# Linear attention with butterfly FFN on one core: second batch's keys taken by VectorE, down butterfly spread over slots 1 to 14, x in 2 KB pieces, first slots reordered

## What is computed

```python
q, k, v = split(x @ W_qkv)                      # per head: 64 wide
q = relu(q @ W_f + b_f);  k = relu(k @ W_f + b_f)
kv = sum_n k[n]^T v[n];  norm = q . sum_n k[n] + 1e-6
x1 = layernorm(x + concat(q @ kv / norm) @ W_out + b_out)
h  = gelu(butterfly(x1 @ W_exp + b_exp, up_weights) + up_bias)
y  = butterfly(h, down_weights) @ W_con + b_con + down_bias
out = layernorm(x1 + y)
```

## Time and profile before

| what | us |
|---|---|
| median of 3 runs (lowest, highest) | 335.33 (334.68, 337.5) |
| the profiled execution | 335.18 |
| its span in the profile | 333.3 |
| TensorE busy in the span | 312.0 (94%) |
| VectorE busy | 242.5 (73%) |
| ScalarE busy | 160.1 (48%) |
| GpSimd busy | 88.0 (26%) |

### The profile page before, as it was taken

One profiled execution on the slowest core, in us unless ns is written; L12 is line 12 of the kernel. 1 busy time (PEld: TensorE's weight loads), 2 busy tenths in 40 slices (PEclk: granted clock), 3 DMA queues, 4 the chain that ended last, 5 costly groups with the idle time before them and its releaser, 6 DMA issues.

```text
span 333.3 us, 5119 instructions
## 1 busy us (share of the span) xinstructions
PE 312.0 (94%) x1813; PEld 218.1 (65%) x1813; DVE 242.5 (73%) x480; ACT 160.1 (48%) x284; POOL 88.0 (26%) x100
## 2 busy tenths in 40 slices
PE   4999799999989999999999999999999898999882
PEld 4876467766757767676777776667777666454471
DVE  2659999868599999778872996397839626477645
ACT  2633245444544445454542656346848845341351
POOL 4059999970000002100200220023004103111222
PEclk9999999999999999999999999999999999999998
DMA  6993244566701900730092006600380390840102
GB/s 181 267 314 132 78 150 154 163 219 148 171 2 38 219 0 5 180 74 0 7 208 46 0 3 147 140 0 2 99 192 3 78 209 6 189 125 2 31 1 63
DMA packets 25616, 33.72 MB, mean 101 GB/s; under 512 B 4184, under 2 KB 14456, under 8 KB 25592
## 3 DMA queue, kind: packets, MB, share of 16 engines
q1 hardware_dynamic: 25432, 33.38, 38.5%
q10 hardware_dynamic: 160, 0.03, 0.0%
HBM read 31.04 MB, written 2.36 MB: 100 GB/s over the span
## 4 chain that ended last, share of the span: by engine, by line
PE 74%; DVE 12%; DMA 4%; issue 4%; ACT 2%; SPq 2%; POOL 1%; POOLq 0%; DVEq 0%; ACTq 0%
PE ring L605 26%; PE kx_ps L692 12%; PE attn_ps L605 8%; PE ring L790 6%; PE ring L712 4%; PE attn_ps L742 4%; PE desk L614 3%; DMA x<-_L_ffn_down_weights_dram 2%; PE desk L726 2%; PE desk L701 2%; DVE qn L1274 2%; PE ring L672 1%; SPq L479 1%; DVE late L1160 1%; DMA q<-in_L_attn_W_qkv_dram 1%
## 5 line engine op out<-in xcount | busy, mean ns | idle before, releaser
L957 ACT ACTIVATE q<-ring,bf_col 128x512 f32<-128x512 f32 x64 | 43.8, 685 | 44.5 <-PE ring L605 43.7
L557 POOL TENSOR_TENSOR var_eps<-mean_var,ln_eps 128x4 f32<-128x4 f32 x14 | 7.1, 505 | 210.8 <-DVE mean_var L1287 210.8
L692 PE MATMUL kx_ps<-k,xs 128*128 128x512 f32 x128 | 60.1, 592 | 0.0
L943 ACT ACTIVATE qn_h<-qn 128x512 fp32r<-128x512 f32 x48 | 29.5, 625 | 27.7 <-DVE qn L1274 27.7
L1274 DVE TENSOR_TENSOR qn<-q,recips 128x512 f32<-128x512 f32 x64 | 41.0, 680 | 1.6 <-DMA recips<-recip_rows 1.6
L549 POOL TENSOR_TENSOR y<-hid,y_up 128x512 f32<-128x512 f32 x18 | 33.7, 1891 | 16.4 <-DMA hid<-in_L_ffn_up_weights_dram 15.4
L605 PE MATMUL ring<-xT_h,wq_h 128*128 128x512 f32 x64 | 35.5, 555 | 0.0
L692 PEld LDWEIGHTS kx_ps<-k,xs 128*128 128x128 f32 x128 | 23.9, 189 | 17.7 <-issue 15.4
L1142 DVE TENSOR_TENSOR qn_l<-qn,qn_h 128x512 fp32r<-128x512 f32 x48 | 32.1, 678 | 4.5 <-ACT qn_h L943 4.3
L1240 DVE TENSOR_TENSOR k_total<-k_total,k 128x1024 f32<-128x1024 f32 x24 | 34.8, 1449 | 0.6 <-ACT k L950 0.4
L1214 DVE TENSOR_TENSOR k<-ring,bf_minus 128x512 f32<-128x512 f32 x32 | 21.9, 684 | 16.5 <-PE ring L605 16.5
(11 more groups left out here) (176 smaller groups left out, 576.8 us busy)
## 6 DMA issues: line engine op xcount, KB each, us to landing
recips<-recip_rows SPq DMA_DIRECT2D x64, 256.0 KB, 5.2
hid<-in_L_ffn_up_weights_dram SPq DMA_DIRECT2D x9, 512.0 KB, 4.2
x<-_L_ffn_down_weights_dram SPq DMA_DIRECT2D x9, 512.0 KB, 6.1
xs<-in_L_attn_x_dram SPq DMA_DIRECT2D x4, 512.0 KB, 6.3
out_dram<-y SPq DMA_DIRECT2D x7, 256.0 KB, 4.0
q<-in_L_attn_W_qkv_dram SPq DMA_DIRECT2D x2, 512.0 KB, 7.3
q<-in_L_attn_W_qkv_dram SPq DMA_DIRECT2D x2, 256.0 KB, 3.5
q<-in_L_attn_W_out_dram SPq DMA_DIRECT2D x2, 256.0 KB, 8.3
```

The source lines that it names most:

```text
L692: t_.matmul(kx_ps[half], xs[b % XBUF][:, t, :], k[kt % KRING][:, half * CH:(half + 1) * CH], start=t == 0, stop=t == TILES - 1).then_inc(s ...
L943: a_.activation(dst, src, ACT.Copy).then_inc(done, 1)
L957: a_.activation(q[:, i % QRING, :], bank(("q", i))[:, :], ACT.Relu, bias=bf_col[:, :])\
```

## The change

1. BARE goes from 16 to 8: batch 1's 16 key halves too have no bias matmul and are taken by k_max on VectorE, and batch 1's kx and key sum end as batch 2's do.
2. The nine down steps lie in slots 1, 2, 3, 5, 6, 8, 10, 12, 14 (before: 1, 2, 3, 5, 6, 7, 8, 9, 10). Steps from PS_LAST (7) on use GpSimd's term buffers `term_up`. The bias steps move from slots 10 to 13 to 13 to 15, their transpose from 14 to 16. By L191 x of (2, 1), transposed in slot 14, now goes to the desk.
3. The copies of V and of all four vo parts go to ScalarE.
4. x and out are seen with four tokens on a partition in a row, so pieces are 2 KB and not 512 B.
5. The start: half of x of batch 0 is loaded first and transposed first; b_f's row is loaded from ScalarE's queue; slot 0 takes over the second half of x and the transposes of the q weights, and project_k(1, 0) comes ahead of their folds.

```diff
-    DOWN_STEP_SLOT = {1: 0, 2: 1, 3: 2, 5: 3, 6: 4, 7: 5, 8: 6, 9: 7, 10: 8}
+    DOWN_STEP_SLOT = {1: 0, 2: 1, 3: 2, 5: 3, 6: 4, 8: 5, 10: 6, 12: 7, 14: 8}
-    BIAS_SLOT = {10: [0, 1], 11: [2, 3], 12: [4, 5], 13: [6]}
-    BIAS_T_SLOT = 14
+    BIAS_SLOT = {13: [0, 1], 14: [2, 3], 15: [4, 5, 6]}
+    BIAS_T_SLOT = 16
...
-    BARE = 2 * TILES
+    BARE = TILES
...
-    xs_view = x.rearrange("b (t p) c -> b p t c", p=128)
-    out_view = out.rearrange("b (h t p) c -> (b h) p t c", p=128, h=CHUNKS)
+    xs_view = x.rearrange("b (h p t) c -> b p h t c", p=128, h=CHUNKS)
+    out_view = out.rearrange("b (h p t) c -> (b h) p t c", p=128, h=CHUNKS)
...
+            load_x(0, slice(0, 1), s_xs0)
             for half in range(2):
                 cols = slice(HD + half * CH, HD + (half + 1) * CH)
                 sp.dma_start(wqkv_raw[:, cols], W_qkv[:, cols]).then_inc(s_wk[half], 16)
-            sp.dma_start(xs[0][:, :, :], xs_view[0, :, :, :]).then_inc(s_xs[0], 16)
-            sp.dma_start(bf_row[:, :], b_f.rearrange("(o n) -> o n", o=1).to_broadcast([128, D])).then_inc(s_bf, 16)
+            load_x(0, slice(1, 2), s_xs[0])
...
             pe.wait_ge(s_const, 2)
+            pe.wait_ge(s_xs0, 16)
+            transpose_tiles(kx_ps[0], lambda i: xs[0][:, i, :]).then_inc(s_xp, 1)
             transpose_weights(2, ring[0]).then_inc(s_wT, 1)
             transpose_weights(3, ring[1]).then_inc(s_wT, 1)
...
-            pe.wait_ge(s_xs[0], 16)
-            transpose_tiles(kx_ps[0], lambda i: xs[0][:, i, :]).then_inc(s_xp, 1)
-            transpose_tiles(kx_ps[1], lambda i: xs[0][:, QUADS + i, :]).then_inc(s_xp, 1)
-            transpose_weights(0, desk).then_inc(s_dmade, 1)
-            transpose_weights(1, ring[2]).then_inc(s_wT, 1)
-            pe.wait_ge(s_wh, 2)
-            pe.wait_ge(s_wl, 2)
+            pe.wait_ge(s_wh, 1)
+            pe.wait_ge(s_wl, 1)
...
+                if s == 0:
+                    pe.wait_ge(s_xs[0], 16)
+                    transpose_tiles(kx_ps[1], lambda i: xs[0][:, QUADS + i, :]).then_inc(s_xp, 1)
+                    pe.wait_ge(s_wh, 2)
+                    pe.wait_ge(s_wl, 2)
                 for kt in k_tiles(s)[:1]:
                     project_k(kt, 1)
                 if s == 0:
+                    transpose_weights(0, desk).then_inc(s_dmade, 1)
+                    transpose_weights(1, attn_ps).then_inc(s_wT, 1)
+                    project_k(1, 0)
...
+                if s in V_SLOT:
+                    act.wait_ge(s_dmade, desk_of["v", V_SLOT[s]] + 1)
+                    a_.activation(wT[:, (4 + V_SLOT[s]) * CH:(5 + V_SLOT[s]) * CH], desk[:, :],
+                                  ACT.Copy).then_inc(s_dtaken, 1)
...
                 if s == 3:
-                    act.wait_ge(s_fold, 5)
-                    a_.activation(vo[:, 0:4, :].rearrange("p a m -> p (a m)"), attn_ps[:, :], ACT.Copy).then_inc(s_voa, 1)
+                    for half, fold in enumerate([attn_ps, spare_ps]):
+                        act.wait_ge(s_fold, 5 + half)
+                        a_.activation(vo[:, 4 * half:4 * half + 4, :].rearrange("p a m -> p (a m)"), fold[:, :],
+                                      ACT.Copy).then_inc(s_voa, 1)
...
+                if n >= PS_LAST:
+
+                    dve.wait_ge(s_up, 3 * STAGES)
+                    terms = term_up
```

More of the change, by code:

```diff
@@ L421, in weights, with load_x @@
                 sp.dma_start(wqkv_raw[:, cols], W_qkv[:, cols]).then_inc(done, 16)
+            def load_x(b, chunks, done):
+                dst = xs[b][:, :, :].rearrange("p (h t) c -> p h t c", h=CHUNKS)
+                sp.dma_start(dst[:, chunks, :, :], xs_view[b, :, chunks, :, :]).then_inc(done, 16)
+            load_x(0, slice(0, 1), s_xs0)
             for half in range(2):
@@ L453, in _ @@
             load_down(0)
-            sp.dma_start(xs[1][:, :, :], xs_view[1, :, :, :]).then_inc(s_xs[1], 16)
+            load_x(1, slice(0, CHUNKS), s_xs[1])
+            for h in range(2):
+                sp.dma_start(bf_col[h * D:(h + 1) * D, :], b_f.rearrange("(p o) -> p o", o=1)).then_inc(s_bfc, 16)
             load_down(1)
@@ L954, in q_relu @@
                 act.wait_ge(s_made, ring_of["q", i] + 1)
+                if i == 0:
+                    act.wait_ge(s_bfc, 32)
                 if i >= QRING:
@@ L1027, in yT_copy @@
                 a_.activation(yT[:, :], bank(("down", n))[:, :], ACT.Identity, bias=bdn_col[:, :]).then_inc(s_taken, 1)
+            act.wait_ge(s_xp, 1)
+            hi(xT_h[:, 0, 0:CH], kx_ps[0], s_xTh)
             act.wait_ge(s_wT, 1)
             a_.activation(wT[:, 2 * CH:3 * CH], ring[0][:, :], ACT.Copy).then_inc(s_wTa, 1)
[L1031 to L1036, removed]
+            act.wait_ge(s_fold, 1)
+            hi(wk_h[:, 0:CH], attn_ps[:, :], s_wh)
+            act.wait_ge(s_bf, 16)
             act.wait_ge(s_bfz, 1)
@@ L1073, in _ @@
                 if s == 0:
-                    for half, fold in enumerate([attn_ps, spare_ps]):
+                    act.wait_ge(s_wT, 3)
+                    a_.activation(wT[:, CH:2 * CH], attn_ps[:, :], ACT.Copy).then_inc(s_wTa, 1)
+                    k_relu(1, 0)
+                    for half, fold in enumerate([spare_ps, attn_ps]):
                         act.wait_ge(s_fold, half + 3)
@@ L1325, in _ @@
             v.memset(wout_diag, 0.0).then_inc(s_zero, 1)
+            dve.wait_ge(s_xTh, 1)
+            lo(xT_l[:, 0, 0:CH], kx_ps[0], xT_h[:, 0, 0:CH], s_xTl)
             dve.wait_ge(s_wT, 2)
             v.tensor_copy(wT[:, 3 * CH:4 * CH], ring[1][:, :]).then_inc(s_wTd, 1)
-            for half, fold in enumerate([attn_ps, spare_ps]):
-                cols = slice(half * CH, (half + 1) * CH)
-                dve.wait_ge(s_wh, half + 1)
-                lo(wk_l[:, cols], fold[:, :], wk_h[:, cols], s_wl)
-            dve.wait_ge(s_xTh, 1)
-            lo(xT_l[:, 0, 0:CH], kx_ps[0], xT_h[:, 0, 0:CH], s_xTl)
+            dve.wait_ge(s_wh, 1)
+            lo(wk_l[:, 0:CH], attn_ps[:, :], wk_h[:, 0:CH], s_wl)
             dve.wait_ge(s_bfh, 2)
```

61 lines of the change are left out of this document (29 added, 32 removed).

## The result

The changed kernel takes 356.68 us (median of 4 runs, 355.97 to 357.84), the kernel before, on the same chip, 335.25. The ratio is 1.0613, 95% interval 1.0567 to 1.0658. The change costs 21.4 us; I had forecast 7.2 (342.5, range 336 to 346.5). The sign and the places were right, the size was a third of what came. Runs over 1.5% above the fastest of their own kernel are left out of the ratios, though not of the medians: 1119.53 us once in f1, 354.42 in f2, 340.08 in f4.

What follows compares the result with a forecast made beforehand. TensorE bounds the whole, but VectorE, nearly full too, sets the pace in slots 4 to 16. Slot 17 comes 7.6 us later (143.3, not 135.7), the last store gives back 0.3: 335.2 + 7.6 - 0.3 = 342.5 us, range 336 to 346.5.

Steps and rivals of the forecast that it cites:

- a sum that gave 142.6: Slot 17 of TensorE: VectorE's start 49.8, plus work 82.5, idle time 9.8 and 0.5 us.
- a walk that gave 144.0: Slots 4 to 16 followed slot by slot in code order, with waits of both engines; slot 17 at 144.0 us.
- Term (d), the start: Start of the kernel: transposing half of x before the weights wins 0.5 us, bounds -1.5 and +1.
- VectorE's work: Slots 4 to 16: 82.5 us, up from 71.7, with k_max at 0.60 us each, or 1.13 for eight beside GpSimd.
- The queue step: Slots 8 to 10, SyncE: spread(0) waits behind load_down(7), beginning near 77.5 us; normalise_q(0) starts at 85.5 to 86.5.
- the list of signs: What would show the forecast right or wrong, among them VectorE over 90% busy in slots 12 to 16.
- VectorE's idle time: Slots 4 to 16: waits for norm, recips and key products, 2.5 + 2.3 + 3.1 + 1.9 = 9.8 us.
- What TensorE saves: Bias matmuls 3.7, V wait 1.7, slot 11 wait 1.4, start 0.5, last store 0.3: 7.6 us if VectorE followed.
- Rival 1: Slots 4 to 16: VectorE packs, idle about 3 us or less, slot 17 near 135 or earlier; chance 0.10.
- rival 2: Slots 4 to 16: VectorE idle 3 to 6 us, slot 17 at 136 to 139, time 335 to 338; chance 0.16.
- Rival 3: Late throughout: k_max slowed beside GpSimd (+4.2), key weights late at the start (+2), 347 to 349 us; chance 0.06.
- Rival 4: The bias products stay, or VectorE's part is wholly hidden in idle time; no chance of its own given.

Runs made afterwards that it cites:

- f1: Changed kernel with the second batch's keys back on ScalarE (BARE 16) and down and bias steps in their old slots: 334.93 us, ratio 0.9955.
- f2: Changed kernel with load_down(7) moved behind spread(0) in SyncE's list, nothing else: 351.59 us, ratio 1.0388.
- f4: Kernel before, with only the V and vo copies on ScalarE and x and out in 2 KB pieces: 336.59 us, ratio 1.0004.
- e4: Changed kernel with the start of before (x of batch 0 whole, behind the key weights): 355.24 us, ratio 1.0557.
- e1: Changed kernel with 59 matmuls that nobody reads put into TensorE's stalls in slots 4, 11, 15 and 16: 350.56 us, ratio 1.0412.
- g3: Kernel before, with only the second batch's keys moved to VectorE (BARE 8, constants made in slot 3): 345.1 us, ratio 1.0273.
- e2: Changed kernel with the second batch's keys back on ScalarE with the bias matmul (BARE 16), thinned steps kept: 350.06 us, ratio 1.0415.
- g1: Changed kernel with BARE 16, thinned steps kept, load_down(7) behind spread(0) and down step 8 in slot 13: 341.07 us, ratio 1.0134.
- g2: Changed kernel with down steps 5 and 6 in slots 7 and 9 and step 8 in slot 13: 345.3 us, ratio 1.0265.
- g4: f1 with down step 8 in slot 11 instead of 10: 333.45 us, ratio 0.9918 against the kernel before.

## Why the prediction was right in kind and wrong in size

I had slot 17 of TensorE at 143.3, between a sum that gave 142.6 and a walk that gave 144.0; it began at 156.48. From there the delay was carried to the end as I had said: 20.8 us at slot 17, 21.9 in the profiled execution. Of the 13.9 us beyond the sum, 4.0 are in VectorE's start, 1.2 in its work and 8.5 in its idle time, together 13.7.

**Term (d), the start: wrong.** I took 0.5 us won (bounds -1.5 and +1). Slot 1 came 2.45 later. The 256 KB of x ahead of the key weights pushed the second half of these from 5.45 to 8.36, and TensorE, full before from there on, waited 2.76 us for it. That is 3 us off the term and outside its bounds. A part of it is chance: in the ten profiles with the new start slot 1 begins between 20.5 and 22.3 (half of them before 21.5), in the four with the old one between 19.4 and 20.5, so the usual loss is nearer 1.7. In the time e4 won back 1.4 us. That the 256 KB on the DMA engines are what holds the key weights up is argued, not shown.

**VectorE's start of slot 4: 53.77, not 49.8.** In e4, with the old start, the same k_max starts at 51.81, so 2.0 of the 4.0 come from the new start; the other 2.0 I haven't traced.

**VectorE's work: right.** 82.5 us forecast for slots 4 to 16, 83.67 measured. k_max takes 684 ns on average over all 48, and 0.68 and 0.69 at 53.77 and 60.69, where GpSimd is busy. So the price of 0.60 start to start, and not the bound of 1.13, holds. As in the prediction, this agrees with the rule of the Trainium skill, SBUF — State Buffer, section Who interferes with whom, by which a VectorE instruction with one SBUF input doesn't contend with GpSimd: k_max has one source in PSUM and one in SBUF.

**The stalls of TensorE: right, where they had a price.**

| where | forecast | measured |
|---|---|---|
| slot 4, k_max behind down step 2 | 3.6 | 4.17 |
| slot 11, step 6 ahead of add_attn(0) | 4 | 4.40 |
| slot 10, the desk behind m_lo(0,0) | named, no price | 1.97 |
| slot 15, x(2,1) at the desk | 4 | 4.47 |
| slot 16, the copy of wdn | 3 | 2.19 |
| wait of VectorE for recips | 2.6 to 3.6 | 3.10 |

The queue step was right in kind: spread(0) stood behind load_down(7) and started 5.0 us behind the reciprocal at 79.40 (SyncE's queue in the changed kernel, to set beside the earlier trace rows); the walk had 5 us between them (72.5 to 77.5), the list of signs 3 to 4:

```profile
84.40 1.82 SPq L478 DMA_DIRECT2D recip_rows<-recip  x4
```

One sign was missed narrowly: VectorE was busy 42.83 of 48.70 us from slot 12 to 16, 88% and not over 90%. The first up product came at 164.84, not at about 150.

**VectorE's idle time: the step that failed.** I wrote "Idle in all 2.5 + 2.3 + 3.1 + 1.9 = 9.8 us" and had only the latencies of norm, the recips and a key product in two places in it. Measured up to the copy of wdn it is 18.3 us (101.95 us from 53.80 to 155.75, less 83.67 of work). The forecast waits all came: 1.79 for norm (2.5 forecast), 2.42 ahead of slot 10 (2.3), 3.10 for the recips (3.1), 3.27 in slot 11 (1.9). What the sum lacks is first of all VectorE waiting for key products right behind the stall of slot 4 (timeline of VectorE in the changed kernel):

```profile
60.69 0.69 DVE L1245 TENSOR_TENSOR k<-ring,bf_minus 128x512 f32<-128x512 f32 x1 [4.03 <-PE ring L612]
```

I had let TensorE catch up at once after each stall, at 0.23 us a matmul. In truth it ran at 0.42 for some microseconds behind each long stall, and so VectorE, which had just been what TensorE waited for, now waited for TensorE. The product for the 4.03 us wait began its last matmul 5.7 us behind the end of the stall (54.50 to 60.22); in e1, where the stall was filled, it was 3.0 (53.28 to 56.27). So 2.7 of the 4.03 are the clock, and the rest is TensorE's other work in between. All waits of VectorE for key products are 13.6 us in six; 2.45 of them lie behind the copy of wdn, and 4.2 were in the forecast. There was no term for the low clock in the sum. e1 prices it in the time: with the stalls filled, 6 us come back. By the rows the stretches ahead of slot 17 cost TensorE 6.7. How the rest of the idle time that wasn't forecast (0.7 for the next key product, 1.4 more in slot 11, 0.8 behind the stall of slot 15, 0.8 for y_bias, small gaps) divides between the clock and lateness going round wasn't taken apart.

**What TensorE saves** was right term by term (16 matmuls, the V wait, the 1.4 near slot 11), and worth nothing here, as the walk said: g3 shows it for the 16 matmuls, and f4, where the V wait went and no time was won, for the V wait.

**The rivals.** Rival 1 (VectorE packs, 332 to 335) is excluded, and so is rival 2 (idle time of 3 to 6 us): no wait of the walk stayed away, and VectorE's idle time was 18.3 us. Rival 3, late throughout and worse, was the nearest (347 to 349), but not by its mechanism: k_max wasn't slowed, and only its late key weights were right. What made it worse was mostly the clock, which no rival had. Rival 4 (the bias products stay) fell with the 16 matmuls that are gone.

**The reason itself.** The prediction put the loss down to VectorE being full, with the links of the chain as its places. e2 shows that the balance is the other way: the thinned steps cost 13 to 15 us and the extra work 7 to 9. In g1, 9 us of the 15 hang on two single links, and g2 gets rid of two stalls by placing steps 5, 6 and 8 otherwise, with the same work on VectorE.

Two things stay open: why the low stretches last as long as they do, and about 2 of the 6 us that g1 still costs over f1.

## What to carry to other kernels

In this kernel a long stall of the engine that bounds it was paid twice, as waiting and as slow work behind it: 18.0 us of waits brought about 8.0 us more (the 6.7 and 1.3 above), so by this kernel a wait of about 4 us on TensorE is to be entered at about one and a half times its length, with a wide margin (f2's two waits of 2.9 and 3.4 brought nothing). Where it can't be avoided, matmuls that nobody reads were better than rest (e1), if they end before the wait does. When a step is moved to a later slot, list what stood behind it in every queue and which bank it now shares (here SyncE's list, the desk, the first add_attn): two such links cost 9.0 us, as much as all the added work (6.6 to 9.4). And take work off the bounding engine only where the one that receives it is idle in that stretch; 3.7 us saved on TensorE cost 9.4 here. The fastest kernel (g4) has one step moved by one slot to where its data is there; that this step is what made it faster than f1 isn't certain.

## What the runs showed of the hardware that I had not expected

The granted clock of TensorE fell to its lower level (1.2 GHz) in each stall of 4.2 to 4.5 us in the changed kernel, not behind it: 3.1, 1.3 and 2.0 us after the engine had stopped (at 53.43, 97.82 and 135.36). It rose again 5.7, 3.7 and 4.4 us after the engine was at work; each low stretch is 6.8 us long. With the wait of only 2.19 us in slot 16 it fell 0.1 us after the wait had ended, for 3.4 us (155.83 to 159.25). In g1, g2 and g3 it also fell beside single waits of 2.4 and 2.5 us. In e4 and f2 the stall of 4.4 us in slot 15 brought only 3.4 us at the lower level. After stalls of 2.9 and 3.4 us in f2's profile it didn't fall (1.00 in both windows). So in these kernels the length of a wait alone decides neither whether the clock falls nor for how long.

The Trainium skill, TensorE: Matmul & The Clock Gate, section Part 1: The HAM clock gate (the "warmup" mystery), puts the lower level down to idle time of TensorE and says that the number of matmuls that one kernel starts with at that level differs from run to run. The rows here agree with the first. As to the second, the runs show such a spread in the middle of a kernel: f2 had a mean granted clock of 0.988 at 347.52 us, 0.979 at 351.97 and 0.973 at 351.20.

TensorE did 59 matmuls more in e1 and the kernel became 6 us faster.
